# Turning the gated activations of an MLP: TensorE transposes replaced by VectorE blocks of 32x32 and SBUF-to-SBUF transfers

## The reference, cut to what matters

```python
# first layer: a gated MLP in which half of the gate is set to zero, row by row
s = silu(x @ w_gate.T)                      # 2048 x 2752
k = int(0.5 * I)
_, idx = top_k(-abs(s), k)                  # the k smallest magnitudes of each row
s[row, idx] = 0.0
h = s * (x @ w_up.T)                        # 2048 x 2752
x = layernorm(x + h @ w_down.T)             # w_down: 1024 x 2752
# second layer: a gated MLP with tiled weights and low-rank terms
x = layernorm(x + ffn(x, ...))
```

## Time and profile before

| | |
|---|---|
| median of three runs | 1946.39 us (1945.27 to 1946.66) |
| profiled execution | 1946.1 us |
| its span in the trace | 1944.3 us |
| granted TensorE clock | 0.999 of full speed |
| busy share: PE, DVE, POOL, ACT | 99%, 64%, 47%, 38% |
| moved by DMA | 203.67 MB, 105 GB/s on average |

### The profile page before, as it was taken

The page is one execution under the profiler, slowest core; times in us unless marked ns, Lnnn a source line. Parts: engine busy times, 40 slices in busy tenths (PEclk is TensorE's granted clock), DMA queues, the critical chain, the costliest instruction groups (busy, mean ns, idle before and its releaser), DMA issues. The chain is left out here.

```text
span 1944.3 us, 24669 instructions
## 1 busy us (share of the span) xinstructions
PE 1923.8 (99%) x9320; PEld 1615.7 (83%) x9320; DVE 1239.7 (64%) x1823; ACT 731.3 (38%) x1184; POOL 916.7 (47%) x705
## 2 busy tenths in 40 slices
PE   9999999999999999999999999999999999999998
PEld 8898878988889888888888988889888777887776
DVE  2147885689864326897532489866017998469963
ACT  4347433573333335523243473333242332113312
POOL 5456894455545544555464455544572331013310
PEclk9999999999999999999999999999999999999999
DMA  4333332334344333434243334343643132212212
GB/s 146 91 102 96 113 110 83 91 98 141 101 124 133 94 89 106 141 98 132 83 139 96 99 97 141 95 130 90 188 147 97 45 129 95 75 48 76 98 44 87
DMA packets 102114, 203.67 MB, mean 105 GB/s; under 512 B 11492, under 2 KB 27876, under 8 KB 100688
## 3 DMA queue, kind: packets, MB, share of 16 engines
q1 hardware_dynamic: 97384, 185.28, 31.0%
q10 hardware_dynamic: 4608, 16.78, 2.2%
HBM read 185.24 MB, written 16.78 MB: 104 GB/s over the span
## 5 line engine op out<-in xcount | busy, mean ns | idle before, releaser
L512 POOL TENSOR_TENSOR wl<-w_in_place,wh 128x512 fp32r<-128x512 f32 (+2 forms) x552 | 721.1, 1310 | 645.9 <-ACT wh L619 645.8
L619 ACT CAST wh<-w_in_place 128x512 fp32r<-128x512 f32 (+2 forms) x560 | 328.4, 589 | 763.6 <-DMA w_in_place<-in_wu 296.9
L1329 PE MATMUL banks<-wh,xTh 128*128 128x512 f32 (+2 forms) x1536 | 566.0, 368 | 5.2 <-POOL wl L512 5.2
L1331 PE MATMUL banks<-wh,xTl 128*128 128x512 f32 (+2 forms) x1536 | 563.4, 367 | 0.0
L1330 PE MATMUL banks<-wl,xTh 128*128 128x512 f32 (+2 forms) x1536 | 563.2, 367 | 0.0
L1329 PEld LDWEIGHTS banks<-wh,xTh 128*128 128x128 f32 x1536 | 288.4, 188 | 47.1 <-POOL wl L512 7.5
L1331 PEld LDWEIGHTS banks<-wh,xTl 128*128 128x128 f32 x1536 | 288.3, 188 | 40.1
L1330 PEld LDWEIGHTS banks<-wl,xTh 128*128 128x128 f32 x1536 | 288.4, 188 | 39.6
L1329 PE MATMUL banks<-wh,hTh 128*128 128x512 f32 x672 | 262.6, 391 | 1.5 <-POOL wl L512 1.5
L1331 PE MATMUL banks<-wh,hTl 128*128 128x512 f32 x672 | 261.5, 389 | 0.0
L1330 PE MATMUL banks<-wl,hTh 128*128 128x512 f32 x672 | 261.5, 389 | 0.0
(11 more groups left out here) (144 smaller groups left out, 2184.3 us busy)
## 6 DMA issues: line engine op xcount, KB each, us to landing
w_in_place<-in_wd SPq DMA_DIRECT2D x176, 256.0 KB, 2.6
w_in_place<-in_wg SPq DMA_DIRECT2D x128, 256.0 KB, 2.6
w_in_place<-in_wu SPq DMA_DIRECT2D x128, 256.0 KB, 2.6
w_in_place<-in_w SPq DMA_DIRECT2D x54, 256.0 KB, 2.9
x_in_place<-in_xT SPq DMA_DIRECT2D x32, 256.0 KB, 3.8
y<-in_xtok SPq DMA_DIRECT2D x4, 2048.0 KB, 8.1
x<-y ACTq DMA_DIRECT2D x16, 512.0 KB, 4.1
xa<-x SPq DMA_DIRECT2D x16, 512.0 KB, 4.2
```

What stands on the lines that cost most here:

```text
L512: nc.gpsimd.tensor_tensor(lo, landed, hi.bitcast(F32), ALU.subtract).then_inc(done, 1)
L619: nc.scalar.copy(hi, piece).then_inc(hi_done, 1)
L1329: nc.tensor.matmul(dst, ah, bh, start=start, stop=False)
L1331: return nc.tensor.matmul(dst, al, bh, start=False, stop=stop)
```

## The change

The turn is taken from PE. DVE transposes every 32x32 block of a chunk in place of its partition quadrant and writes it to `squares` (over `hTh`). Sixteen SBUF-to-SBUF transfers a chunk, from SP, move quadrant g of `squares` part a to quadrant a of `landed` part g (over `hTl`): each is 32 partitions by one run of 2 KB (1.5 KB in the two narrow chunks). They go out four behind each of four weight pieces. ACT casts `landed` to `hTh`, one quarter of a chunk behind each of four weight pieces; DVE subtracts in place to get `hTl`, one chunk later than before. The order of the down stage starts with chunk 3, then 4, 5, 0, 1, 2, and PE waits for `t_lo` there. The small loads of the last down stage move two to ten pieces later. The host lays the tokens of a tile out in another order, outside the measured time.

```diff
-D_ORDER = SETS[NJ - 2][::-1] + list(range(SETS[NJ - 2][0] - 1, YC - 1, -1)) + SETS[NJ - 1][::-1] + list(range(YC - 1, -1, -1))
+J_Y = next(j for j in range(NJ) if SETS[j][-1] >= YC)
+J_ORDER = list(range(J_Y, NJ)) + list(range(J_Y - 1, -1, -1))
+D_ORDER = [c for j in J_ORDER for c in SETS[j][::-1]]
+Y_USED = 2 * (NC - SETS[J_Y][0])
...
+SENT_0 = (16, 20, 24, 32, 36, 43)
+CAST_0 = (21, 25, 29, 37, 41, 47)
+def sent_at(b, n):
+    first = SENT_0 if b == 0 else [KH * (j + 2) - 1 for j in range(NJ)]
+    return [(j, n - f) for j, f in enumerate(first) if f <= n < f + GROUPS]
+def cast_at(b, n):
+    first = CAST_0 if b == 0 else [KH * (j + 2) + 2 for j in range(NJ)]
+    return [(j, n - f) for j, f in enumerate(first) if f <= n < f + NT]
...
+        squares = sb("squares", [P, NC * TB], F32, 4, offset=at["hTh"])
+        landed = sb("landed", [P, NC * TB], F32, 4, offset=at["hTl"])
...
+            def send_squares(b, n):
+                for j, g in sent_at(b, n):
+                    if g == 0:
+                        sp.wait_ge(squares_done, NT * (NJ * b + j + 1))
+                        sp.sem_inc(passed_sp, 1)
+                    for a in range(GROUPS):
+                        sp.dma_start(h_part(landed, j, g)[SQ * a:SQ * (a + 1), :],
+                                     h_part(squares, j, a)[SQ * g:SQ * (g + 1), :]).then_inc(t_in[j % 2], 16)
             def load_up(b):
                 for i in range(NG):
                     load_gu(wu, up_at(b), i)
+                    if b:
+                        send_squares(b, i)
...
             for d in range(ND):
                 load_d(NB - 1, d)
+                send_squares(NB - 1, NG + d)
...
-                if d == 8:
+                if 12 <= d < 18:
+                    load_b((d - 12) // 2, d % 2)
+                if d == 18:
                     load_small()
-                if 10 <= d < 16:
-                    load_b((d - 10) // 2, d % 2)
-                if d in (14, 16):
-                    load_xa(0, (d - 14) // 2)
-                if d == 24:
+                if d in (20, 22):
+                    load_xa(0, (d - 20) // 2)
+                if d == 26:
                     x_tiles(NB - 1)
...
-            def turned(b, j, p):
-                for m, c in enumerate(SETS[j]):
-                    act.wait_ge(t_done, NC * b + c + 1)
-                    if c == YC and b:
-                        act.wait_ge(x1_out, 16 * NT * b)
-                    nc.scalar.copy(hTh[:, c, :], banks[2 * m + p][:, :]).then_inc(t_hi, 1)
+            def turned(b, n):
+                for j, g in cast_at(b, n):
+                    if g == 0:
+                        act.wait_ge(t_in[j % 2], 16 * GROUPS * GROUPS * (NJ // 2 * b + j // 2 + 1))
+                    nc.scalar.copy(h_part(hTh, j, g), h_part(landed, j, g)).then_inc(t_hi, 1)
...
                         V.tensor_tensor(s, banks[2 * t + j % 2][:, 0:width(j)], s, ALU.mult).then_inc(u_freed, 1)
+                    turn(b, j)
                     if j < NJ - 1:
                         masked(b, j + 1)
                     if j == 0:
                         norm_bias(b - 1)
-                    turned(b, j, j % 2)
+                    else:
+                        turned(b, j - 1)
...
+            def turn(b, j):
+                if b and j == J_Y:
+                    dve.wait_ge(x1_out, 16 * NT * b)
+                    dve.sem_inc(passed_dve, 1)
+                o, n = SETS[j][0] * TB, len(SETS[j]) * TB
+                into = squares[:, o:o + n].rearrange("p (a c u) -> p c a u", a=GROUPS, u=P)
+                for t in range(NT):
+                    dve.wait_ge(u_freed, 8 + 4 * NJ * b + 4 * j + t + 1)
+                    src = w0[:, in_chunk(j, t)] if b == 0 else v[:, t, cols(j)]
+                    full, tt = width(j) // P, slice(SQ * t, SQ * (t + 1))
+                    ins = V.transpose(into[:, 0:full, :, tt],
+                                      src[:, 0:full * P].rearrange("p (c a u) -> p c a u", a=GROUPS, u=SQ))
...
+                    ins.then_inc(squares_done, 1)
+            def turned(b, j):
+                for g in range(NT):
+                    dve.wait_ge(t_hi, NT * (NJ * b + j) + g + 1)
+                    V.tensor_tensor(h_part(hTl, j, g), h_part(landed, j, g), h_part(hTh, j, g).bitcast(F32),
+                                    ALU.subtract).then_inc(t_lo, 1)
...
-                def inside(j, i):
-                    if j and i == 3:
-                        turn(b, j - 1, (j - 1) % 2)
                 for j in range(NJ):
-                    if j >= 2:
-                        turned(b, j - 2)
-                    chunk(b, up_at(b), j, u_done, lambda t: waits(j, t), lambda i: inside(j, i))
+                    chunk(b, up_at(b), j, u_done, lambda t: waits(j, t))
             def down(b, bank_waits):
...
+                    j = next(j for j in range(NJ) if c == SETS[j][-1]) if any(c == m[-1] for m in SETS) else None
+                    if n == 0 and j is not None:
+                        pe.wait_ge(t_lo, NT * (NJ * b + j + 1))
+                        pe.sem_inc(passed_pe, 1)
...
-            turn(NB - 1, NJ - 1, 1)
-            down(NB - 1, lambda t, n: turned(NB - 1, NJ - 2 + n))
+            down(NB - 1, lambda t, n: taken_up(NB - 1, 4 * (NJ - 2 + n) + t + 1))
```

More of the change, by code:

```diff
@@ L40 @@
 TAIL = I - (NC - 1) * P
+SQ = 32
+GROUPS = P // SQ
 RING = 5
@@ L312, in program @@
         u_done, u_freed = sem("u_done"), sem("u_freed")
-        t_done, t_hi, t_lo = sem("t_done"), sem("t_hi"), sem("t_lo")
+        squares_done, t_hi, t_lo = sem("squares_done"), sem("t_hi"), sem("t_lo")
+        t_in = [sem(f"t_in{i}") for i in range(2)]
         d_done, d_evac = sem("d_done"), sem("d_evac")
@@ L350, in cols, with h_part, h_tile @@
             return slice(FIRST[j], FIRST[j] + width(j))
+        def h_part(h, j, g):
+            n = len(SETS[j]) * P
+            o = SETS[j][0] * TB + g * n
+            return h[:, o:o + n]
+        def h_tile(h, c, g):
+            j = next(j for j in range(NJ) if c in SETS[j])
+            m = c - SETS[j][0]
+            return h_part(h, j, g)[:, m * P:(m + 1) * P]
         @block.sync
@@ L689, in up @@
                         high_gu(up_at(b), KH * j + i)
-                        if i == KH - 1 and j:
-                            turned(b, j - 1, (j - 1) % 2)
+                        turned(b, KH * j + i)
                     if j == 1:
@@ L753, in gate_1 @@
                             copy_u(NJ - 1)
[L754 to L759, removed]
+                        turned(0, KH * j + i)
             def down_then_up(b):
@@ L1120, in take_up @@
                         norm_bias(b - 1)
-                    turned(b, j, j % 2)
[L1123 to L1129, removed]
-                for m, c in enumerate(SETS[j]):
-                    rows = P if c < NC - 1 else TAIL
-                    dve.wait_ge(t_hi, NC * b + c + 1)
-                    V.tensor_tensor(hTl[0:rows, c, :], banks[2 * m + p][0:rows, :],
-                                    hTh[0:rows, c, :].bitcast(F32), ALU.subtract).then_inc(t_lo, 1)
+                    else:
[12 more added lines that the diff above has]
+                                      src[:, 0:full * P].rearrange("p (c a u) -> p c a u", a=GROUPS, u=SQ))
+                    if width(j) % P:
+                        step(ins)
+                        for a in range(0, GROUPS, 2):
+                            ins = V.transpose(into[:, full, a:a + 2, tt],
+                                              src[:, full * P:width(j)].rearrange("p (a u) -> p a u", u=SQ))
+                            if not a:
+                                step(ins)
+                    ins.then_inc(squares_done, 1)
[4 more added lines that the diff above has]
+                                    ALU.subtract).then_inc(t_lo, 1)
             def mask_w0(j):
@@ L1149, in _ @@
             search(0)
-            mask_w0(0)
+            for j in range(2):
+                mask_w0(j)
+                turn(0, j)
             for j in range(NJ - 2):
                 take_gate(1, j)
-                turned(0, j, j % 2)
-                mask_w0(j + 1)
-            mask_w0(NJ - 1)
-            turned(0, NJ - 2, 1)
+                mask_w0(j + 2)
+                turn(0, j + 2)
+                if j:
+                    turned(0, j - 1)
+            turned(0, NJ - 3)
             take_gate(1, NJ - 2)
-            turned(0, NJ - 1, 0)
+            turned(0, NJ - 2)
+            turned(0, NJ - 1)
             take_gate(1, NJ - 1)
@@ L1350, in chunk @@
                     ins.then_inc(pe_used, 1)
-                    if inside is not None:
-                        inside(i)
-            def turn(b, j, p):
-                pe.wait_ge(u_freed, 8 + 4 * NJ * b + 4 * (j + 1))
-                pe.sem_inc(passed_pe, 1)
-                for m, c in enumerate(SETS[j]):
-                    for t in range(NT):
```

(11 more changed lines are left out.)

72 lines of the change are left out of this document (34 added, 38 removed).

## The result

The changed kernel takes **1928.01 us** in the median of 4 runs (1926.88 to 1929.76), the kernel before beside it 1945.96 (1945.27 to 1946.66): a ratio of 0.9908, 95% interval 0.9896 to 0.9921, 18 us less. The forecast was 36 us less, 1910. The sign and the stated range (1903 to 1934) held; half of the gain is missing, and the forecast's own range without its rivals, 1903 to 1920, did not hold. The profiled execution is the one of 1926.88 us, its span 1925.0.

The account below looks back on a forecast made before the run. PE was taken to bound the kernel: 1946.1 less 40.9 for transposes and 0.7 for a wait, plus 5 of new waits, gives 1910 us. Range 1903 to 1934, held 8 in 10; 1903 to 1920 without rivals.

Parts of the forecast that it names:

- What bounds the kernel: PE, busy in 99% of the span, sets the time; taking 368 transposes at 0.111 us off it saves 40.9 us.
- DVE: In up(2)'s stretch DVE has 85.4 us of work in 94.1, 91%: transposes 0.68 us each, four subtractions 4.0.
- the rival at 2028: Slower: 32x32 blocks don't stream, 3.2 us a transpose instruction, DVE falls behind in up stages and gate(1); chance 0.11.
- the one of DVE too full: At 1.8 us a transpose DVE lags in the up stages and gate(1), giving 1922 us; chance 0.10.
- SP and its queue: On SP, five issues of 0.33 us behind one piece take 1.65 us, just fitting the narrowest piece's 1.76; no stall.
- twice that as the upper bound: Four transfers delay the landing of the piece behind by about 1.1 us; over 32 partitions at most twice that, at least 0.
- The new waits: SP's wait for squares and ACT's for landings stay inside margins; passages, down(3) and strays cost PE 3 + 1 + 1 = 5 us.
- the passages: At up(1)-gate(2) and up(2)-gate(3), POOL fully busy and held up by DVE's subtractions: 1.5 us each, bounds 0 and 3.5.
- The margins of 6.3 and 2.8 us: Free time of a weight piece issued four pieces ahead, after landing, cast and subtraction: 6.3 us, at least 2.8 in narrow chunks.
- transfers that crowd the weights: Rival: the transfers cost PE 1 us a chunk, 24 us in all, giving 1934 us; chance 0.07.
- DVE's share between the multiplies, above 85%: Sign of being right: DVE busy above 85% between first and last multiply, with transposes near 0.7 us.
- PE waiting for POOL behind late landings in every chunk: Sign of being wrong: weights landing late make PE wait for POOL's low parts in every chunk.

Follow-up runs that it names:

- one issue a piece: Changed kernel with each of the 96 pieces of h sent in one transfer of 128 partitions instead of four of 32; h^T not the transpose: 1906.81 us.
- the kernel that halves them: Changed kernel with two of the four transfers of each piece of h issued by ScalarE (ACT) instead of SP, nothing left out: 1915.78 us.
- eight issues: Changed kernel with each transfer of 32 partitions split in two of 16, 768 issues, same bytes, nothing left out: 2112.58 us.

## Why the prediction was half right

- **What bounds the kernel**: right. 368 transposes off PE are worth 39.9 us (40.9 forecast) by the kernel that leaves three quarters of them out.
- **DVE**: right to 3% in the stretch (82.5 us against 85.4), both terms a little high: 0.62 us a transpose where they overlap and 3.9 us for four subtractions, against 0.68 and 4.0. The blocks stream, so the rival at 2028 fell, and the one of DVE too full with it. No transpose was held up by POOL: the maximum is 703 ns, 4% over the mean of 677 at 512 columns, while the two-input subtraction beside it goes up to 1793. By the rule of the Trainium skill, "SBUF — State Buffer", section "SBUF: two separate sides", that was to be expected, and this trace agrees.
- **SP and its queue**: here is the step that failed. "An issue takes 0.33 us", and from it "behind one piece SP has 5 x 0.33 = 1.65 us ... It just fits". That row is a load of 128 partitions out of HBM; the new transfers, SBUF to SBUF over 32, take 0.59 to 0.60, and the load behind four of them 0.51. The sum is 4 x 0.60 + 0.51 = 2.9 us, more than a piece of any width. The prediction allowed for 32 partitions where it put bounds on the landing ("twice that as the upper bound") and none where it costed the issue. Twice 0.33 there too would have given 4 x 0.66 + 0.33 = 2.97 us, and a rival of its own.
- **The new waits**: SP never waited for `squares_done`, and the passages do wait, as said; the weight was off. The margins of 6.3 and 2.8 us were used as if whole; SP's bursts eat them first, and with them the cover for slow landings: they count 2.6 and 2.2 us, the load at the passage took 5.6. 5 us were allowed; with one issue a piece about 1 us is lost (1906.8 against 1905.8), with the real issues 22.
- **The range**: 1928 lies in it by luck. It reached up to 1934 for DVE's fullness and for transfers that crowd the weights, and neither happened; an issue longer than 0.33 us was no part of it.
- **The rivals**: the one of transfers that crowd the weights gave 1934 at 1 us a chunk, the nearest in effect (22 us in 24 chunks), but by landings, whose bytes are worth 3.4 us. It got 0.07. The rule cited there, of the Trainium skill, "SBUF — State Buffer", section "Door 1: The DMA port swizzle", is one of bytes; since the bytes hardly counted, no run here shows whether it holds.
- **What would show it**: DVE's share between the multiplies, above 85%, came (82.5 of 96.5 us), and the mean transpose of 512 columns is 0.68 us. "PE waiting for POOL behind late landings in every chunk" was the sign named for wrong, and half of it came: 30 places in all, 17 more than before, most of the new ones in the narrow chunks and at the passages.

## What to carry to other kernels

A transfer is first an instruction of the queue that issues it. Price it from a row of its own kind (partitions, source, and what stands behind it), and where the trace has none, put the same bounds on the issue as on the landing. Then set a burst of issues against the lead that the loads behind it have in hand, stretch by stretch, not their sum against a whole chunk. Where a wait ends in a cast, follow it back past the engine that the page names until one is found that was never idle, and look at a late load twice: when it was issued, and how long it took to land.

## What the runs showed of the hardware

- An SBUF-to-SBUF issue over 32 or 16 partitions takes 0.51 us alone and 0.59 to 0.62 in a row, whether it moves 8 bytes or 2 KB a partition; over 64 partitions 0.46 to 0.59; over 128, 0.47. More transfers for the same bytes cost in full, and smaller ones are not cheaper. Single ones take much longer: the slowest of 384 took 2.33 us, of the 384 with 8 bytes on the kernel before 2.01.
- A load of 128 partitions behind a pack of them takes 0.51 us to issue in place of 0.33. Why, no run shows.
- Issues on SP's and ACT's queues overlap: in the kernel that halves them the median is 0.58 us on SP and 0.61 on ACT, against 0.59 on SP alone.
- The granted clock fell to its lower level (0.53, 0.54 and 0.57 in three stretches of 3.5 to 3.6 us) behind waits of 1.1 and 1.8 us, of 3.0 us, and of 2.6 us, so that a wait can cost PE more than its own length: with eight issues the waits for POOL sum to 138.8 us, but the kernel is 206 us slower than with one. It did not fall behind every such wait: behind the 2.52 us at 982.59 in the changed kernel, and behind 1.54 us with one issue a piece, matmuls kept their 0.39 us.
